# Attention and expert kernel: the weighted sums of tile 0 two steps later, x loaded ahead of tile 1, expert weights loaded over tiles 1 to 4

## The reference

```python
c = layernorm(x)
s = (c @ w_c + b_c)[:, :, None] + (q @ w_q + b_q)[:, None, :] + einsum('bcd,bqd,d->bcq', c, q, w_cq) + b_cq
a = softmax(s, axis=2)                      # over the 6404 context rows
c2q = einsum('bcq,bqd->bcd', a, q)
b_att = softmax(max(s, axis=2), axis=1)
q2c = einsum('bc,bcd->bd', b_att, c)[:, None, :]
x = x + concatenate([c, c2q, c * c2q, c * q2c]) @ W_l.T + b_l
n = layernorm(x)
expert = argmax(n @ wr + br)
x = x + (gelu(n @ w1[expert] + b1[expert]) @ w2[expert] + b2[expert])
```

## Time and profile before

| | |
|---|---|
| median of 3 runs | 250.81 us (249.9 to 254.19) |
| the profiled execution | 252.84 us, span 251.1 us |
| PE busy | 202.9 us (81%) |
| DVE busy | 182.7 us (73%) |
| ACT busy | 156.3 us (62%) |
| POOL busy | 119.6 us (48%) |
| mean granted TensorE clock | 0.922 |
| data moved by DMA | 51.78 MB, mean 206 GB/s |

### The profile page before, as it was taken

One profiled execution on the slowest core, in us unless ns is written; L12 is line 12 of the kernel. 1 busy time (PEld: TensorE's weight loads), 2 busy tenths in 40 slices (PEclk: granted clock), 3 DMA queues, 4 the chain that ended last, 5 costly groups with the idle time before them and its releaser, 6 DMA issues.

```text
span 251.1 us, 4978 instructions
## 1 busy us (share of the span) xinstructions
PE 202.9 (81%) x1833; PEld 148.9 (59%) x1833; DVE 182.7 (73%) x400; ACT 156.3 (62%) x246; POOL 119.6 (48%) x173
## 2 busy tenths in 40 slices
PE   0289839999988805999999999979997298799970
PEld 0134326665655502667666676769995297799960
DVE  2999894479993107979989989995886627576770
ACT  2832896099594502977977879978911336566640
POOL 3791718005300199079492399764400470016773
PEclk9999977799999955899999999999999569999995
DMA  6999969379999706999999999998998149999100
GB/s 221 384 255 265 236 145 198 84 157 214 201 262 223 181 0 152 162 250 245 207 271 204 246 221 232 224 210 195 200 250 242 42 152 356 311 382 381 62 22 0
DMA packets 141102, 51.78 MB, mean 206 GB/s; under 512 B 121108, under 2 KB 138917, under 8 KB 141078
## 3 DMA queue, kind: packets, MB, share of 16 engines
q1 hardware_dynamic: 140144, 50.08, 86.9%
q0 software_dynamic: 784, 1.38, 1.5%
q10 hardware_dynamic: 150, 0.00, 0.0%
HBM read 10.74 MB, written 3.75 MB: 58 GB/s over the span
## 4 chain that ended last, share of the span: by engine, by line
DVE 32%; issue 24%; PE 16%; DMA 11%; POOL 8%; ACT 5%; another core or an unknown queue 1%; DVEq 0%; POOLq 0%; ACTq 0%
DMA PT<-Phl 10%; DVE Phl L786 9%; DVE S L769 7%; POOL out_x L581 4%; PE psO L1038 3%; ACT Phl L639 3%; ACT S L624 2%; PE psS L1018 2%; PE psS L1019 2%; PE psS L1020 2%; DMA S<-in_x 2%; PE psO L1040 1%; DVE st L703 1%; PE psS L1242 1%
## 5 line engine op out<-in xcount | busy, mean ns | idle before, releaser
L769 DVE TENSOR_SCALAR_CACHE_REDUCE S<-psS 128x1024 f32<-128x1024 f32 x48 | 58.1, 1216 | 23.7 <-POOL Phl L507 12.8
L624 ACT ACTIVATE S<-S,negb 128x1024 f32<-128x1024 f32 x48 | 55.0, 1145 | 29.9 <-DVE negb L777 29.9
L786 DVE TENSOR_TENSOR Phl<-S,Phl 128x1024 f16<-128x1024 f32 x39 | 52.0, 1333 | 10.0 <-ACT Phl L639 9.9
L639 ACT CAST Phl<-S 128x1024 f16<-128x1024 f32 x48 | 50.2, 1045 | 9.9 <-DMA PT<-Phl 8.6
L1018 PE MATMUL psS<-qT,gh 128*128 128x512 f16 x96 | 38.7, 404 | 13.9 <-DVE S L769 10.6
L507 POOL TENSOR_TENSOR Phl<-S,Phl 128x256 f16<-128x256 f32 x36 | 23.5, 684 | 50.5 <-ACT Phl L639 50.5
L1038 PE MATMUL psO<-qn,PT 128*128 128x256 f16 x204 | 39.7, 288 | 5.3 <-DMA PT<-Phl 5.2
L1019 PE MATMUL psS<-qT,gh 128*128 128x512 f16 x96 | 38.7, 403 | 0.0
L1020 PE MATMUL psS<-qT,gl 128*128 128x512 f16 x96 | 38.6, 402 | 0.0
L1038 PE MATMUL psX<-qn,PT 128*128 128x256 f16 x204 | 36.3, 273 | 2.4 <-DMA PT<-Phl 1.2
L1040 PE MATMUL psO<-qn,PT 128*128 128x128 f16 x204 | 37.8, 228 | 0.0
(11 more groups left out here) (232 smaller groups left out, 414.8 us busy)
## 6 DMA issues: line engine op xcount, KB each, us to landing
PT<-wp SPq DMA_DIRECT2D x8, 512.0 KB, 7.0
stageT<-in_ctxT SPq DMA_DIRECT2D x6, 512.0 KB, 7.2
qn<-wp SPq DMA_DIRECT2D x6, 512.0 KB, 8.7
wp<-in_w SPq DMA_DIRECT2D x4, 512.0 KB, 5.0
stageT<-in_w SPq DMA_DIRECT2D x4, 512.0 KB, 4.6
rows_by_expert<-stageT SPq DMA_DIRECT2D x4, 385.5 KB, 5.1
S<-rows_by_expert SPq DMA_DIRECT2D x2, 514.0 KB, 7.2
S<-rows_by_expert SPq DMA_DIRECT2D x2, 385.5 KB, 6.8
```

What stands on the lines that cost most here:

```text
L624: nc.scalar.activation(slot(t, e), slot(t, e), ACT.Exp, bias=negb[:, t:t + 1], accum_out=Lp[:, t * NG + e:t * NG + e + 1]).then_inc(exp_do ...
L639: nc.scalar.copy(hi, slot(t, e)).then_inc(high_done, 1)
L769: nc.vector.tensor_scalar(out=into, in0=bank(u, n)[:, 0:into.shape[1]], scalar1=1.0 / GS, scalar2=None, op0=ALU.mult, op1=ALU.max, accum_o ...
L786: nc.vector.tensor_tensor(lo, slot(t, e), hi, ALU.subtract).then_inc(low_done, 1)
```

## The change

Three things move; no instruction is added or taken away.

- TensorE: the weighted sums of tile 0 follow the general rule. Before, `weighted(0, e)` stood behind the scores of (1, e + 3); now it stands behind the scores of (1, e + 5), and from there on in tile 2.
- SyncE: the load of `x_re` stands ahead of all transposes of tile 1. Before, it stood behind the third transpose of tile 2. The loads of w1 pieces 2 and 3 and of the four w2 pieces stand at (1, 3), (2, 1), (2, 5), (3, 3), (4, 1) and (4, 5), each behind the transpose of that tile and piece. Before, they stood at (1, 0), (1, 3), (1, 5), (2, 5), (3, 5) and (4, 5).
- GpSimd: the three instructions that build `pick` come ahead of `low_piece(1, 3)` instead of behind it.

```diff
--- before.py
+++ after.py
@@ -410,15 +410,17 @@
             for e in range(1, NG):
                 transpose(0, e)
 
+            sp.dma_start(x_re, x.rearrange("(t p) d -> p t d", p=P)).then_inc(x_re_landed, 16)
+
+            W1_BEHIND = {(1, 3): 2, (2, 1): 3}
+            W2_BEHIND = {(2, 5): 0, (3, 3): 1, (4, 1): 2, (4, 5): 3}
             for t in range(1, T):
                 for e in range(NG):
                     transpose(t, e)
-                    if t == 1 and e in (0, 3):
-                        load_w1(2 + e // 3)
-                    if t == 2 and e == 2:
-                        sp.dma_start(x_re, x.rearrange("(t p) d -> p t d", p=P)).then_inc(x_re_landed, 16)
-                    if e == 5 and t <= H:
-                        load_w2(t - 1)
+                    if (t, e) in W1_BEHIND:
+                        load_w1(W1_BEHIND[t, e])
+                    if (t, e) in W2_BEHIND:
+                        load_w2(W2_BEHIND[t, e])
 
             sp.wait_ge(empty_ready, 2)
             for k in range(FILLS):
@@ -528,7 +530,6 @@
             pool.wait_ge(empty_ready, 1)
             nc.gpsimd.iota(empty[:, 2 * D:ROW].bitcast(I32), pattern=[[0, 1]], base=NOWHERE,
                            channel_multiplier=0).then_inc(empty_ready, 1)
-            low_piece(1, 3)
             then(nc.gpsimd.memset(pick[:, :, :], 0.0))
             for r in (0, 32):
                 then(nc.gpsimd.affine_select(out=pick[:, :, :], in_=pick[:, :, :], compare_op=ALU.not_equal, fill=1.0,
@@ -550,6 +551,7 @@
                                                    parts[:, 0, at + a:at + a + CHUNK], ALU.subtract)
                 last.then_inc(w_low, 1)
 
+            low_piece(1, 3)
             pool.wait_ge(x_re_landed, 16)
             pool.wait_ge(late_landed, 16 * NLATE)
             nc.gpsimd.tensor_tensor(x_re, x_re, blr[:, :].unsqueeze(1).broadcast_to([P, T, D]),
@@ -1067,13 +1069,7 @@
                         row_terms()
                     for c in range(2 * n, min(2 * n + 2, NCH)):
                         scores(u, c)
-                    if u == 1:
-                        if n >= 3:
-                            weighted(0, n - 3)
-                    elif u == 2 and n < AHEAD:
-                        if n < 3:
-                            weighted(0, NG - 3 + n)
-                    elif n >= AHEAD:
+                    if n >= AHEAD:
                         weighted(u - 1, n - AHEAD)
                     elif u > 1:
                         weighted(u - 2, NG - AHEAD + n)

```

## The result

The changed kernel takes 235.46 us (median, 234.88 to 236.31); the kernel before, run beside it, 251.61 us. The ratio is 0.938 with a 95% interval of 0.931 to 0.945. Measured once more later, the same changed kernel took 235.87 us, ratio 0.935 (0.930 to 0.941). The profiled execution took 235.85 us with a span of 234.1, so 17.0 us less than the 252.84 and 251.1 of before. 232.9 us was forecast. The time is inside the range of 228.5 to 239.5 us, but 0.5 us above the band of 231 to 235 us that was given 0.56; it lies in the band of the second rival, 235 to 240 us, that was given 0.23.

What follows compares the result with a forecast made beforehand. TensorE's own work was taken to bound the steady part, behind a stall for x. Tile 2's copy at 45.7 plus 86.9 us puts tile 7's at 132.6 instead of 150.51; 250.81 - 17.9 = 232.9 us, range 228.5 to 239.5.

Steps and rivals of the forecast that it cites:

- the second rival: Tiles 2 to 7: the DMA engines set the time, 91 to 93 us for the stretch, 237 to 239 us; chance 0.23.
- The stall: GpSimd's 21.5 us wait for reloaded x and VectorE's 12.8 us wait behind it would go with x loaded earlier.
- the stall stays: Rival: something other than x holds GpSimd at the addition, only the start gains, about 246 us; chance 0.04.
- The opening: Up to tile 2's first scores copy: later sums of tile 0 bring it from 51.98 to 45.7 us, gain 6.3 us.
- the charge for the row terms: TensorE in tile 1, behind the scores of piece 4: row terms take 2.12 us, to 37.8 us.
- The stretch: Tile 2's first scores copy to tile 7's: five tiles at 16.54 us plus 4.2 us for seven loads, 86.9 us.
- The 0.6 us for each load: Tiles 2 to 7: each load among the transposes adds 0.6 us, seven loads 4.2 us.
- a sign of being wrong: Middle part: waits for transposed pieces on TensorE or ScalarE adding up to more than some 5 us.
- TensorE alone: Rival for tiles 2 to 7: loads hide fully behind 82.7 us of matmuls, 228.7 us; chance 0.13 for below 231.
- The DMA engines bound the stretch: Rival for tiles 2 to 7: at 219 to 225 GB/s it takes 91 to 93 us, 237 to 239 us; chance 0.23.
- The slower case: Rival: spread loads drop the engines to 190 GB/s, 20.4 MB take 107.4 us, 253.4 us in all; chance 0.04.

Runs made afterwards that it cites:

- e2: The kernel before with only the load of x moved ahead of the transposes of tile 1: 239.39 us, ratio 0.955.
- e1: The kernel before with only the weighted sums of tile 0 two steps later, x and weight loads as before: 245.72 us, ratio 0.979.
- e12: The changed kernel measured once more, unedited: 235.87 us, ratio 0.935.
- e6: The changed kernel with the six late weight loads cut from 512 KB to 64 KB, leaving out most expert weights: 232.13 us, ratio 0.914.
- e9: The changed kernel with the six weight loads cut to 64 KB and eight idle matmuls in TensorE's gap in the opening: 231.23 us, ratio 0.919.
- e5: The changed kernel with eight idle matmuls in TensorE's gap ahead of the scores of tile 1, piece 4: 239.13 us, ratio 0.951.
- e7: The changed kernel with the row terms one piece earlier, in TensorE's gap ahead of the scores of tile 1, piece 4: 236.15 us, ratio 0.936.
- e3: The kernel before with later sums of tile 0 and x ahead of tile 1, weight loads left where they were: 235.14 us, ratio 0.935.

## Why the prediction was right, and where it was off

**The stall.** It was caused by the place of the load of x in SyncE's queue, and all of it went: e2 alone gives 12.7 us, e1 keeps the stall. The case "the stall stays" is refuted.

**The opening.** I took 45.7 us for the copy of tile 2, between 44.9 and 46.1. The two profiled executions of the changed kernel have 47.50 and 44.30, both outside. The step that failed is the charge for the row terms: I took 2.12 us at either clock, "both ends differ only by the clock", but let the clock slow only the matmuls around them. At 0.50 they take 3.96 us. At the fast end the sum let them start at 35.7 us, where the scores end at half clock; in e12 they started at 34.84. Which clock comes was not known either: 45.7 us lies between the two measured, and neither had it. The reading that TensorE's waits for the first transposed piece cause VectorE's two waits was right; they shrank from 3.37 and 3.55 us to nothing and 1.59, where at most 0.5 was forecast.

**The stretch.** 86.9 us forecast, 85.74 and 87.68 measured. TensorE's 16.54 us a tile are confirmed by e6 and e9 to 0.1 us. The 0.6 us for each load were near in the sum (4.2 us, against 3.0 and 5.0) and wrong as a mechanism; that the sum came so near is luck. They were also misread. The tile of 16.59 us was taken as one without a load, but SyncE's timeline of the kernel before has a load in each of the three tiles from which the 0.6 us were read:

```profile
103.24 0.57 SPq L401 DMA_DIRECT2D stageT<-in_w  x1
120.18 0.57 SPq L401 DMA_DIRECT2D stageT<-in_w  x1
136.82 0.57 SPq L401 DMA_DIRECT2D stageT<-in_w  x1
```

The copies on VectorE also move against TensorE's work: TensorE's own starts are 16.79 and 16.91 us apart where the copies are 17.21 and 16.59. In the changed kernel the loads of tile 2 cost nothing. TensorE waits 1.28 us, until 103.52, for the piece behind the load of tile 3, and 0.89 us, until 118.49, for a piece behind the first load of tile 4; the two tiles took 1.45 and 1.05 us more than 16.52. For the middle the prediction had named a sign of being wrong, waits for transposed pieces of more than some 5 us in all. They were 2.2 us on TensorE and 3.6 on ScalarE (5.8 together) in the first profiled execution, and 5.2 and 7.2 in e12, so the sign was there.

**The rivals.** "TensorE alone" would need free loads; e6 shows that they cost about 3 us in the stretch. "The DMA engines bound the stretch" with its 237 to 239 us was too strong for the time but right for the margin: what TensorE wins in the opening is taken back by waits for transposed pieces (e5, e7, e12), and not when the loads are small (e9). The slower case stayed away. Over the whole stretch the busy times of the changed kernel give 226 GB/s (last column), well above the 195 below which it would have decided:

```profile
47.50:133.20 85.70, 83.53 (x715) 58.69 (x714) 77.32 (x126) 69.29 (x104) 51.70 (x71) 1.00 1.12 226
```

By this rate the stretch moved 19.4 MB and not the 20.4 of the prediction, since tile 5's last transposes are issued behind tile 7's copy. The Trainium skill ("DMA: Bandwidth & Descriptors", Latency and other measured facts) gives 261 GB/s for a DMA transpose with a non-contiguous middle dimension; this mix of transposes and loads didn't reach it.

**From the profiled execution to the median.** Its sum was 234.9 us, the measured one 235.85: 1.8 us more in the opening, 1.2 less in the stretch, 0.3 more behind. The rest of the 2.6 us between 232.9 and 235.46 is my carrying over of the 2.0 us by which the profiled execution of before lay above its median of three. In the later measurements that median was 251.4 to 252.2, so those three were low and 2.0 us was too much to carry over.

**The spreading.** It had no term of its own, and e3 shows that it needs none. `pick` was not tried alone; it ran in idle time of GpSimd.

## What to carry to other kernels

When a wait has no named releaser, look in the DMA queue for a transfer whose issue plus landing time meets the end of the wait, and ask what stands ahead of its issue in program order: here one 512 KB load behind the third transpose of tile 2 cost 11 to 13 us, and moving one line removed it. Where an engine and the DMA queues both run near their limits, a gain early in the pipeline is worth only what the queue lets through; cut the transfers' bytes in a test kernel before building on it. Look at what stands right behind each plain load in the queue: here a transpose issued less than 2 us behind a 512 KB load landed late, and it cost time where an engine needed it next.

## What the runs showed of the hardware

- A DMA transpose of 128 x 16 x 128 values lands in 4.2 us on the median. At the start of tile 1 it took 3.7 to 3.9 us when issued 2.3 to 2.5 us behind a plain 512 KB load, 6.1 to 6.7 when issued 1.2 to 1.7 us behind it, and 7.8 to 8.4 when issued 0.7 to 1.0 us behind it; in the last case the queue that issued it was held for 4.0 to 5.6 us instead of 1.6. Behind a load of 64 KB, at 0.72 and 0.74 us, it took 4.2 and 3.9 us (e9, e6).
- After the same idle gap of TensorE (2.25 and 2.27 us) the same program once kept the granted clock at 1.00 and once fell to 0.50 from 35 us on. With the gap filled it fell too: with idle matmuls to 0.50 from 38 to 41 us (e5), with the row terms from 33 to 36 us (e7).
- Eight fp32 matmuls of one column with their bias row take 2.12 us at the upper clock and 3.96 us at the lower, 1.87 times as much, though they move almost no columns.
